# Weighted sums of one query tile of a sparse-attention indexer, moved from VectorE to GpSimd

## What is computed

```python
iq = (hidden_states @ idx_wq_w).reshape(b, s, IDX_H, IDX_D)      # 16 heads of 128
ik = hidden_states @ idx_wk_w
iw = hidden_states @ idx_weights_w * IDX_H ** (-0.5)
idx_scores = jnp.einsum('bqn,bnqk->bqk', iw,
    jax.nn.relu(jnp.einsum('bqnd,bkd->bnqk', iq, ik))) * IDX_D ** (-0.5)
idx_scores = jnp.where(causal, idx_scores, -jnp.inf)
_, topk_idx = jax.lax.top_k(idx_scores, TOPK)                     # TOPK = 128
```

## Time and profile before

| | |
|---|---|
| median of three runs | 1475.95 us |
| the profiled execution | 1476.29 us, its span 1474.5 us |
| TensorE busy | 1327.4 us, 90% of the span |
| VectorE busy | 1105.6 us, 75% |
| ScalarE busy | 832.5 us, 56% |
| GpSimd busy | 640.5 us, 43% |
| chain that ended last, by engine | TensorE 68%, VectorE 18%, ScalarE 4%, issue 4%, DMA 2%, GpSimd 2% |
| VectorE's sums of line 1299, whole kernel | 105 instructions, 87.1 us |

### The profile page before, as it was taken

The page is one execution under the profiler, slowest core; times in us unless marked ns, Lnnn a source line. Parts: engine busy times, 40 slices in busy tenths (PEclk is TensorE's granted clock), DMA queues, the critical chain, the costliest instruction groups (busy, mean ns, idle before and its releaser), DMA issues.

```text
span 1474.5 us, 21228 instructions
## 1 busy us (share of the span) xinstructions
PE 1327.4 (90%) x7144; PEld 1105.3 (75%) x7144; DVE 1105.6 (75%) x2233; ACT 832.5 (56%) x1813; POOL 640.5 (43%) x629
## 2 busy tenths in 40 slices
PE   2777999999989789998659999999999999999977
PEld 1656788888789677776348888888888888888866
DVE  5637434433548599999969998898898998898864
ACT  4554442222236556774557767666676767667631
POOL 3421120000027445645556555655666555555522
PEclk9978999999999999998669999999999999999988
DMA  6531220000022334754820000000000000000101
GB/s 217 177 100 51 70 81 0 1 19 1 17 81 64 102 75 122 227 181 140 269 95 14 1 28 28 28 28 28 28 16 12 28 27 28 28 27 15 51 29 58
DMA packets 83722, 95.59 MB, mean 65 GB/s; under 512 B 11680, under 2 KB 59296, under 8 KB 83104
## 3 DMA queue, kind: packets, MB, share of 16 engines
q1 hardware_dynamic: 83616, 94.24, 20.2%
HBM read 75.34 MB, written 18.87 MB: 64 GB/s over the span
## 4 chain that ended last, share of the span: by engine, by line
PE 68%; DVE 18%; ACT 4%; issue 4%; DMA 2%; POOL 2%; SPq 1%; DVEq 1%; ACTq 0%; POOLq 0%
PE ps L328 16%; PE ps L330 15%; PE ps L329 15%; PE ps L1715 8%; PE ps L1735 3%; DVE acc L1299 3%; PE ps L1734 3%; DVE top L1310 2%; DVE xn_l L1361 1%; DVE rop L1322 1%; DVE acc L1313 1%; DVE rop L1320 1%; DVE pm L1349 1%; DVE rop L1321 1%; PE ps L1430 1%
## 5 line engine op out<-in xcount | busy, mean ns | idle before, releaser
L692 POOL TENSOR_SCALAR pm<-pm,smx 128x128 f32<-128x128 f32 (+7 forms) x256 | 190.5, 753 | 214.6 <-DVE smx L1355 214.6
L966 ACT ACTIVATE pm<-pm,smx 128x128 f32<-128x128 f32 (+7 forms) x256 | 197.2, 772 | 39.8 <-DVE smx L1349 38.7
L1349 DVE CUSTOM_DVE_ANT_0 pm<-ps,mbias 128x128 f32<-128x128 f32 (+7 forms) x256 | 191.3, 752 | 34.0 <-PE ps L1715 13.1
L1715 PE MATMUL ps<-ident,pm 128*128 128x128 f32 x1152 | 176.2, 278 | 9.0 <-DVE xn_l L1361 3.5
L972 ACT ACTIVATE xn_h<-ps 128x512 fp32r<-128x512 f32 (+3 forms) x256 | 128.8, 513 | 86.0 <-PE ps L1715 82.9
L1361 DVE TENSOR_TENSOR xn_l<-ps,xn_h 128x512 fp32r<-128x512 f32 (+3 forms) x256 | 144.6, 587 | 26.6 <-ACT xn_h L972 25.6
L328 PE MATMUL ps<-latT_l,qc_h 128*128 128x512 f32 (+3 forms) x384 | 143.1, 373 | 20.5 <-DVE smx L1349 12.5
L1715 PEld LDWEIGHTS ps<-ident,pm 128*128 128x128 f32 x1152 | 133.4, 142 | 35.3 <-issue 12.3
L330 PE MATMUL ps<-latT_h,qc_h 128*128 128x512 f32 (+3 forms) x384 | 134.1, 349 | 0.0
L329 PE MATMUL ps<-latT_h,qc_l 128*128 128x512 f32 (+3 forms) x384 | 133.4, 347 | 0.0
L1299 DVE SCALAR_TENSOR_TENSOR acc<-ps,iw,acc 128x768 f32<-128x768 f32 (+4 forms) x105 | 87.1, 876 | 23.5 <-ACT ps L865 23.3
(11 more groups left out here) (280 smaller groups left out, 3699.1 us busy)
## 6 DMA issues: line engine op xcount, KB each, us to landing
iwq_raw<-in_L_attn_idx_wq_w SPq DMA_DIRECT2D x48, 256.0 KB, 3.2
base<-in_L_ffn_mean_w SPq DMA_DIRECT2D x28, 256.0 KB, 2.8
wring<-in_L_ffn_w SPq DMA_DIRECT2D x24, 256.0 KB, 3.0
ow_raw<-in_L_attn_o_w SPq DMA_DIRECT2D x8, 512.0 KB, 3.9
xn_t<-in_L_attn_o_w SPq DMA_DIRECT2D x8, 512.0 KB, 4.0
wuvo<-pr_even SPq DMA_DIRECT2D x8, 512.0 KB, 4.9
wuvo<-pr_hl SPq DMA_DIRECT2D x8, 512.0 KB, 4.8
wuvo_h<-wuvo SPq DMA_DIRECT2D x16, 256.0 KB, 2.6
```

The lines of the kernel that those rows point to most:

```text
L692: pool.tensor_scalar(pm[:, i % 4, 0:w], pm[:, i % 4, 0:w], smx[:, 32 + i:33 + i], 0.0, ALU.mult, ALU.add).then_inc(hd_p, 1)
L966: act.activation(pm[:, i % 4, 0:w], pm[:, i % 4, 0:w], ACT.Exp, bias=smx[:, i:i + 1], scale=-1.0, accum_out=smx[:, 16 + i:17 + i]).then_in ...
L1349: dve.tensor_tensor_reduce(out=pm[:, i % 4, 0:w], in0=two_banks(2 * (i % 2), w), in1=mbias[:, TRI[t]:TRI[t + 1]], scale=1.0, scalar=3.0 * BIG,
L1715: done = pe.transpose(ps[:, 4 + i % 2, tile(k)], pm[:, tq % 4, tile(4 * c + k)], ident[:])
```

## The change

Tile 4's sums leave VectorE. ScalarE writes the rectified scores of tile 4 to a new SBUF buffer `relu4` of 128 x 640 (it is a single buffer) in place of PSUM. GpSimd multiplies that buffer by the head's weight and adds it to `acc`, in two instructions, `tile4_sum`; for the first head one instruction is enough. ScalarE waits, before it writes the buffer for a head, until the sum of the head before has been made (`ix_a4`). TensorE takes the banks of tile 4 again when ScalarE has read them (`ix_r4`). Tile 5 stays as it was. The new GpSimd call stands behind `index_lo` and `index_weights_lo` of the step after the one whose scores it adds.

```diff
+        relu4 = sbin(r_scope, "relu4", [P, 5 * P])
...
+        def summed(n):
+            return n if n < 48 else 48 + (n - 48) // 2 if n < 80 else n - 16
...
             def drop_later(phase):
-                pool.wait_ge(ix_acc, (48, 80, 112)[phase])
+                pool.wait_ge(ix_acc, (48, 64, 96)[phase])
+                if phase == 1:
+                    pool.wait_ge(ix_a4, IDXH)
...
+            def tile4_sum(head):
+                w = iw[:, 4, head:head + 1]
+                pool.wait_ge(ix_r4, head + 1)
+                if head == 0:
+                    pool.tensor_scalar(acc_of(4), relu4[:], w, 0.0, ALU.mult, ALU.add).then_inc(ix_a4, 1)
+                else:
+                    pool.wait_ge(ix_a4, head)
+                    pool.tensor_scalar(relu4[:], relu4[:], w, 0.0, ALU.mult, ALU.add).then_inc(ix_w4, 1)
+                    pool.wait_ge(ix_w4, head)
+                    pool.tensor_tensor(acc_of(4), acc_of(4), relu4[:], ALU.add).then_inc(ix_a4, 1)
...
                     index_lo(step + 1)
                 if step + 3 < STEPS:
                     index_weights_lo(step + 3)
+                if IDXH < step <= 2 * IDXH:
+                    tile4_sum(step - IDXH - 1)
                 if step in (IDXH, 2 * IDXH):
                     drop_later(step // IDXH - 1)
...
             def index_relu(step):
                 for n, t in index_tiles(step):
                     act.wait_ge(ix_s, n + 1)
-                    act.activation(score(n, t), score(n, t), ACT.Relu).then_inc(ix_r, 1)
+                    if t == 4:
+                        reach(act, ix_a4, step % IDXH)
+                        act.activation(relu4[:], score(n, t), ACT.Relu).then_inc(ix_r4, 1)
+                    else:
+                        act.activation(score(n, t), score(n, t), ACT.Relu).then_inc(ix_r, 1)
...
             def index_sum(step):
                 head, tiles = step % IDXH, index_tiles(step)
+                tiles = [(n, t) for n, t in tiles if t != 4]
...
-                    reach(pe, ix_acc, slot_free(n))
+                    if n < 48:
+                        reach(pe, ix_acc, slot_free(n))
+                    elif n < 50:
+                        pe.wait_ge(ix_acc, 48)
+                    elif t == 4:
+                        pe.wait_ge(ix_r4, step % IDXH)
+                    elif n == 80:
+                        pe.wait_ge(ix_r4, IDXH)
+                    else:
+                        pe.wait_ge(ix_acc, summed(n - 2) + 1)
```

More of the change, by code:

```diff
@@ L297, in build @@
         ik_ld, ik_w, ik_mm, ik_hi, ik_lo = sems("ik_", "ld w mm hi lo")
-        ix_wh, ix_w, ix_q, ix_qhi, ix_qlo, ix_s, ix_r, ix_acc, ix_mask = sems("ix_", "wh w q qhi qlo s r acc mask")
+        ix_wh, ix_w, ix_q, ix_qhi, ix_qlo, ix_s, ix_r, ix_acc, ix_r4, ix_w4, ix_a4, ix_mask = sems("ix_", "wh w q qhi qlo s r acc r4 w4 a4 mask")
         tk_max, tk_rep, tk_mask, tk_last = sems("tk_", "max rep mask last")
@@ L510, in _ @@
                 sp.wait_ge(pr_st[m], 48)
-            sp.wait_ge(ix_acc, 7 * IDXH)
+            sp.wait_ge(ix_acc, 6 * IDXH)
             load_wq(0)
@@ L1291, in index_sum @@
                 head, tiles = step % IDXH, index_tiles(step)
+                tiles = [(n, t) for n, t in tiles if t != 4]
                 for n, t in tiles:
                     w = iw[:, t, head:head + 1]
-                    dve.wait_ge(ix_r, n + 1)
+                    dve.wait_ge(ix_r, summed(n) + 1)
                     if head == 0:
@@ L1297, in index_sum @@
                     else:
-                        dve.wait_ge(ix_acc, n - len(tiles) + 1)
+                        dve.wait_ge(ix_acc, summed(n) - len(tiles) + 1)
                         dve.scalar_tensor_tensor(acc_of(t), score(n, t), w, acc_of(t), ALU.mult, ALU.add)\
@@ L1601, in pair_transposes @@
                 if j == LATER + 1:
-                    pe.wait_ge(ix_acc, 7 * IDXH)
+                    pe.wait_ge(ix_acc, 6 * IDXH)
                 for a in range(4):
```

## The result

| | before | after |
|---|---|---|
| median of the runs, us | 1476.38 (1475.61 to 1476.95, 4 runs) | 1503.61 (1502.88 to 1507.62, 4 runs) |
| profiled execution, its span | 1476.29, 1474.5 | 1502.88, 1501.1 |

The ratio is 1.019, with an interval of 1.0172 to 1.0209. The kernel became 27.2 us slower by the medians and 26.6 by the profiled executions; the forecast was 1506.7, 30.8 slower (28.8 and 2 for the clock).

What follows compares the result with a forecast made beforehand. VectorE was taken to bound the kernel, with 4.68 us a step in phase 1. The profiled 1476.29 + 28.8 of delay + 2 for the clock gave 1507.1, or 1506.7 against the median; range 1501 to 1518.

Steps and rivals of the forecast that it cites:

- The ring: In phase 1 ScalarE and GpSimd wait for each other in a closed loop, 6.55 us a step against 4.68; chance 0.82.
- The addition: GpSimd's adding of 640 columns of tile 4 to `acc` each step, 1565 ns; scaled from the skill page, 1.41 us.
- The multiplication: GpSimd's weighting of tile 4's 128x640 rectified scores each step, 806 ns.
- The wait of GpSimd for itself: On GpSimd, the semaphore wait between multiplying and adding tile 4's scores, 0.15 us a head.
- The step from GpSimd to ScalarE: From the end of the sum on GpSimd to the start of rectifying on ScalarE, 0.03 us.
- The ends: Phase 1's start and end: `index_hi(19)` at 518.70, `index_hi(33)` at 612.9, first round of tiles 4 and 5 at 618.6.
- The term for the clock: TensorE's clock may fall in phase 1, where it works 56% of a step: 2 us taken, 15 at most.
- the chain from there is VectorE without a gap: From the end of phase 1 to 749 us VectorE has no gap, so the 28.8 us delay reaches the end.
- ScalarE's wait: In phase 1 the rectifying of tile 4 waits for GpSimd's addition some 3 us each time.
- Idle time of GpSimd that takes the sums: Rival: GpSimd's idle 2.68 us a step in phase 1 holds the 2.52 us sum, 3 us faster, 1473; chance 0.06.
- The clock that stays down: Rival: TensorE's clock falls in phase 1 and stays low, costing 15 us and a little in phase 2, 1520; chance 0.12.
- Sums and reads that hinder each other: Rival: GpSimd and VectorE both touch `acc` and SBUF in phase 1, 1 us more, 1508; chance within the loop's 0.82.

## Why the prediction was right

**The ring** was the mechanism, and four runs show it: opened in either of two ways it costs nothing (ratios 0.9999 and 1.0001), and shortened by a known piece it shortens by that piece (5.81 and 5.03 a turn). The period was predicted as 6.55 and was 6.52 to 6.56 in steps without a pair.

**Its terms.** The addition: 1565 ns from the line through 512 and 1024 columns, measured 1.54, and 1.57 in the runs with a full GpSimd. The lower estimate of 1.41, scaled from a figure of the page "GPSIMD Engine Reference" of the Trainium skill (section "Performance versus the Vector engine"), was too low for this size. The multiplication: 806 ns, measured 0.81. The wait of GpSimd for itself: 0.15 by the earlier trace rows, measured 0.07 (547.70 to 547.77). The step from GpSimd to ScalarE: 0.03, measured 0.09. These two errors nearly cancel, which is luck.

**The ends.** `index_hi(19)` was predicted at 518.70 and came at 518.06, in an execution that had reached the index 0.8 us earlier. From there to `index_hi(33)` it took 93.67 us, predicted 94.2. The step with `pair_hi` in it took 7.47 (563.82 to 571.29), 0.94 over the turn, predicted 0.95. A step behind a `split_pair` took 6.69, 0.16 over, predicted 0.3. From `index_hi(33)` to the first round it took 6.26 us, predicted 5.7. The round started at 617.99, predicted 618.6. It is this close in part by luck: the earlier arrival took off 0.8 us and the turns 0.5, and the end gave back 0.6 and the start 0.1.

**What was off.** Three things. The term for the clock was mis-sized: 2 us were taken and nothing was measured, for the turn is 6.5 at a granted clock of 1.00 and of 0.74 alike. Against the profiled execution the forecast was 1507.1 - 1502.88 = 4.2 too long, and this is 2 of it; 0.6 is the delay at the end of phase 1 (28.8 against 28.2), and that is no error of the ring, since the execution had arrived 0.8 earlier. The second is the sentence that the chain from there is VectorE without a gap, so that the delay goes through to the end. In phase 2 1.2 us were given back: VectorE had idled there twice before, for 1.38 at 600.39 and for 0.19, and with the change only once, for 0.45. And at the start of the heads nothing waited for VectorE's rounds; the last pair came later than they did, as told above. Since the pairs come just as late by the change (774.13 against 747.45), the delay went through all the same, 26.8 us of it; that part of the forecast was right for another reason than the one given. The third changed no number: ScalarE's wait was said to be some 3 us and is 4.03 in a step without a pair (the prediction's own terms from `index_hi` to the end of the sum, 5.2, less some 1.2 of work on ScalarE, give 4), and TensorE was said to wait for the sums of tile 5, but it waits mostly for the rectifying of tile 4 (31.0 us, 11.6 of them once, against 5.1), since the bank that it writes next is freed by that now.

**The rivals.** Idle time of GpSimd that takes the sums for a gain of 3 us: this is the kernel with the sum first, and it came to 1.0001, not to a gain. Its steps did shorten from 4.68 to 4.37, but each `split_pair` on top costs about 2 us, and the phase is 1.9 us longer. The prediction had allowed for that: with `split_pair` on top it said no change or a loss of 2 to 3 us. The clock that stays down did not come. Sums and reads that hinder each other are at most the 0.03 us between an addition of 1.54 and one of 1.57, and whether that is the cause was not tried.

**What it was worth at best.** The prediction put the length of a step without the sum at no less than 3.7 to 3.8, and it is 3.89. It did not say that a step with a pair and the two behind it would take 14.2 us whatever VectorE is spared. The gain open to any such change is therefore about 4 us and not 14 times 0.8.

## What to carry to other kernels

Idle time of an engine is free only for work that stands where it idles: before moving work, write down for one step what each of the two engines waits for in list order, and look for a ring; its length is the sum of all its parts, and here it was 6.53 us where the fullest engine, GpSimd, has 4.37 of work. If there is one, a second buffer or moving the work ahead of the wait each takes it away whole, so try the order of the list first, since it costs no space. And price the move with the work left out altogether before refining it: here that ceiling was about 4 us, while a stall that had nothing to do with the change held 9. And before comparing start times of two profiles, take off what they differed by ahead of the change: here it was up to 5 us, more than most of the gains.

## What was unexpected of the hardware

- TensorE worked 3.9 of 6.5 us in the change's steps and was mostly granted 1.00, the level of 2.4 GHz (542 to 548.5), with stretches at 0.74 (568 to 574.5). The fall cost nothing in a step with slack, and 1.46 us where a step had none (7.58 us at 0.77 against 6.12 at 1.00, the same work).
- A wait of GpSimd for its own last instruction left 0.07 to 0.09 us here, against 0.15 in the earlier trace rows.
- An activation with a scale per partition over 640 columns took 0.83 us from SBUF to SBUF, where rectifying the same columns from PSUM to SBUF took 0.71; GpSimd's multiplication took 0.80. Moving the multiplication from GpSimd to ScalarE costs no more there than it saves here.
